# W staged in a room of its own, x loaded in halves, adapter units moved in the order

## The reference

```
x, coeff[8], ids[8], mask[8,1024,1024] (0 or 1), W[1024,1024], bias[1024], weight[8,1024,1024]
output = einsum('bsi,oi->bso', x, W) + bias
sign   = 2*mask - 1
diff   = einsum('bsi,bio->bso', x, sign)
x      = x + output + diff*coeff[b]
x      = x + einsum('bsi,boi->bso', x, weight[ids[b]])
```

## Time and profile before

| | us |
|---|---|
| median of three runs | 422.8 |
| the profiled execution's own time | 423.07 |
| its span, first to last instruction | 421.3 |
| TensorE matmuls busy | 390.4 |
| VectorE busy | 366.6 |
| ScalarE busy | 258.0 |
| TensorE busy from 385.3 to 407.0 | 16.66 of 21.70 |

### The profile page before, as it was taken

How to read it: one execution, slowest core, us unless ns; L and a number is a source line. 1 busy time by engine, 2 the same in 40 slices (tenths; PEclk the granted TensorE clock), 3 DMA queues, 4 the chain that set the end, 5 groups by cost and what they waited for, 6 DMA issues and landing times.

```text
span 421.3 us, 6999 instructions
## 1 busy us (share of the span) xinstructions
PE 390.4 (93%) x2496; PEld 354.8 (84%) x2496; DVE 366.6 (87%) x400; ACT 258.0 (61%) x313; POOL 6.0 (1%) x14
## 2 busy tenths in 40 slices
PE   1979749999999999999999999999999999999777
PEld 1878748999899998999999998999999998999655
DVE  0455899999999999999999999999999999998740
ACT  3476765666676766667566766667566676665321
POOL 1111000000000000000000000000000000000000
PEclk9999979999999999999999999999999999999999
DMA  7998996988579874999779995999479975545211
GB/s 225 273 323 285 226 222 167 276 230 222 167 206 286 252 215 126 269 233 237 188 213 244 231 245 167 281 244 239 148 234 271 248 186 172 155 142 174 83 50 50
DMA packets 62451, 88.54 MB, mean 210 GB/s; under 512 B 7122, under 2 KB 48082, under 8 KB 62418
## 3 DMA queue, kind: packets, MB, share of 16 engines
q1 hardware_dynamic: 62418, 88.11, 78.9%
HBM read 79.70 MB, written 8.39 MB: 209 GB/s over the span
## 4 chain that ended last, share of the span: by engine, by line
PE 66%; DVE 18%; ACT 8%; DMA 3%; issue 2%; SPq 1%; ACTq 0%; DVEq 0%
PE first_ps L243 34%; PE second_ps L260 30%; DVE h_lo L396 6%; DVE natural L380 4%; DVE masks L360 4%; ACT masks L290 3%; DVE M_lo L365 2%; PE turn_ps L227 2%; DMA x_nat<-in_x_dram 2%; DVE w_lo L384 2%; ACT h_hi L316 1%; ACT w_hi L305 1%; DMA natural<-in_L_cond_weight_dram 1%; ACT M_hi L297 1%; ACT out_sb L323 1%
## 5 line engine op out<-in xcount | busy, mean ns | idle before, releaser
L243 PE MATMUL first_ps<-x_lo,M_hi 128*128 128x256 f32 x512 | 147.6, 288 | 10.0 <-DVE h_lo L396 6.0
L243 PE MATMUL first_ps<-x_hi,M_hi 128*128 128x256 f32 x512 | 145.6, 284 | 0.0
L243 PE MATMUL first_ps<-x_hi,M_lo 128*128 128x256 f32 x512 | 145.5, 284 | 0.0
L297 ACT CAST M_hi<-masks 128x1024 fp32r<-128x1024 f32 x64 | 67.2, 1050 | 117.6 <-DVE masks L360 117.6
L243 PEld LDWEIGHTS first_ps<-x_lo,M_hi 128*128 128x128 f32 x512 | 98.9, 193 | 13.2 <-issue 6.2
L260 PE MATMUL second_ps<-w_hi,h_lo 128*128 128x512 f32 x256 | 100.2, 391 | 5.0 <-DVE w_lo L384 2.8
L260 PE MATMUL second_ps<-w_hi,h_hi 128*128 128x512 f32 x256 | 99.9, 390 | 0.0
L243 PEld LDWEIGHTS first_ps<-x_hi,M_hi 128*128 128x128 f32 x512 | 98.9, 193 | 1.1
L260 PE MATMUL second_ps<-w_lo,h_hi 128*128 128x512 f32 x256 | 99.6, 389 | 0.0
L243 PEld LDWEIGHTS first_ps<-x_hi,M_lo 128*128 128x128 f32 x512 | 98.8, 193 | 0.0
L360 DVE SCALAR_TENSOR_TENSOR masks<-masks,coeffs,WT 128x1024 f32<-128x1024 f32 x64 | 81.8, 1278 | 13.0 <-ACT masks L290 9.5
(11 more groups left out here) (16 smaller groups left out, 128.1 us busy)
## 6 DMA issues: line engine op xcount, KB each, us to landing
masks<-in_mask_Bx4096x_ik_dram SPq DMA_DIRECT2D x64, 512.0 KB, 6.6
natural<-in_L_cond_weight_dram SPq DMA_DIRECT2D x256, 128.0 KB, 3.8
x_nat<-in_x_dram SPq DMA_DIRECT2D x8, 1024.0 KB, 7.8
out_dram<-out_sb SPq DMA_DIRECT2D x32, 256.0 KB, 3.3
natural<-in_L_cond_W_dram SPq DMA_DIRECT2D x8, 512.0 KB, 7.8
bias_col<-in_L_cond_b_dram SPq DMA_DIRECT2D x4, 1.0 KB, 5.3
coeffs<-in_condB_coeff_dram SPq DMA_DIRECT2D x1, 4.0 KB, 4.7
ids_row<-in_itok_B_dram SPq DMA_DIRECT2D x1, 0.0 KB
```

Source lines behind the costliest of these rows:

```text
L243: done = nc.tensor.matmul(acc(u), left, right, start=(k == 0 and u % 2 == 0 and j == 0), stop=(k == K - 1 and u % 2 == 1 and j == 2))
L297: nc.scalar.copy(by_chunk(M_hi, n), by_quadrant(masks[:, n % RING, :].bitcast(F32))).then_inc(M_hi_done, 1)
```

## The change

W gets room of its own, `W_nat`, 8 slots that lie where the second halves of `w_hi` and `w_lo` will be (`w_hi` and `w_lo` are each split into a tensor for the even and one for the odd half; the first unit of the odd half, g = 4, waits for all eight turns of W). Loads of W and of the first four units wait for no slot of `natural`. x is loaded, and waited for, in two halves of its columns. On TensorE `first(n)` now stands ahead of `turn_W(n+2)`, and turn_x(b+1, 1) stands at the end of slot 7, ahead of second(b-1, 3); its round and rest stand behind `round_h` and `rest_h`. At the start the second half of the first x is turned after first(0). Units 0 to 3 are formed in slots 4 to 7 (before 5 to 8), slot 8 forms none, and from slot 9 the lag is 5 as before. In slot 63 two units are formed, 58 and 59, and the last four are formed after `rest_h(7)` with the turn of a unit ahead of the rest of the one before. ScalarE copies the last tiles out after the last rounding.

```diff
-        w_hi = sb("w_hi", [P, 2, K, HALF], F32R)
-        w_lo = sb("w_lo", [P, 2, K, HALF], F32R)
+        w_hi_even = sb("w_hi_even", [P, K, HALF], F32R)
+        w_lo_even = sb("w_lo_even", [P, K, HALF], F32R)
+        with nc.sbuf_tensor("W_nat", [P, K, D], F32) as W_nat:
+            pass
+        w_hi_odd = sb("w_hi_odd", [P, K, HALF], F32R)
+        w_lo_odd = sb("w_lo_odd", [P, K, HALF], F32R)
...
+        def unit_of(n):
+            return n - 4 if 4 <= n < 8 else n - 5 if n > 8 else None
... SyncE
             load_mask(0)
-            load_x(0)
-            for n in range(1, RING):
-                load_W(n)
-                load_mask(n)
+            load_x(0, 0)
+            load_W(1)
+            load_mask(1)
+            load_W(2)
+            load_mask(2)
+            load_x(0, 1)
+            load_W(3)
+            load_mask(3)
+            load_W(4)
...
-                if n < RING:
-                    sp.wait_ge(W_turned, n + 1)
-                    load_W(n + RING)
                 if n + RING < CHUNKS:
                     sp.wait_ge(M_done, n + 1)
                     load_mask(n + RING)
-                if n in (4, 5):
-                    for g in (2 * n - 8, 2 * n - 7):
-                        sp.wait_ge(W_turned, RING + g + 1)
-                        load_unit(g)
+                if n < 3:
+                    load_W(n + 5)
+                if n in (2, 3, 4, 5):
+                    load_unit(n - 2)
... TensorE
             turn_W(0)
             turn_x(0, 0)
             turn_W(1)
-            turn_x(0, 1)
-            for n in range(CHUNKS + K):
+            for n in range(CHUNKS):
                 b, i = n // K, n % K
+                first(n)
                 if n + 2 < K:
                     turn_W(n + 2)
-                if n < CHUNKS:
-                    first(n)
-                if i == 0 and 1 <= b < B:
-                    turn_x(b, 1)
+                if n == 0:
+                    turn_x(0, 1)
                 if i == 4 and b + 1 < B:
                     turn_x(b + 1, 0)
+                if i == 7 and b + 1 < B:
+                    turn_x(b + 1, 1)
                 if i % 2 and b:
                     second(b - 1, i // 2)
+            for t in range(4):
+                second(B - 1, t)
... ScalarE
             copy_WT(0)
             sign(0)
+            round_M(0)
             round_x(0, 0)
-            round_M(0)
             copy_WT(1)
             sign(1)
-            round_x(0, 1)
...
                 if n + 1 < CHUNKS:
                     round_M(n + 1)
-                if 0 <= n - W_LAG < CHUNKS:
-                    round_w(n - W_LAG)
+                if n == 0:
+                    round_x(0, 1)
+                if n + 2 < K:
+                    copy_WT(n + 2)
+                if g is not None:
+                    round_w(g)
                 if n + 2 < CHUNKS:
                     sign(n + 2)
-                if n + 2 < K:
-                    copy_WT(n + 2)
-                if i == 2 and 1 <= b < B:
-                    round_x(b, 1)
...
-                if i == 7 and b < B:
+                if n == CHUNKS - 1:
+                    round_w(n - 4)
+                if i == 7:
                     round_h(b)
+                    if b + 1 < B:
+                        round_x(b + 1, 1)
+            take_out(B - 2, 3)
+            for g in range(CHUNKS - 4, CHUNKS):
+                round_w(g)
+            for t in range(4):
+                take_out(B - 1, t)
... VectorE
-                if 0 <= g < CHUNKS - 1:
+                if g is not None:
                     add_diagonal(g + 1)
-                if 0 <= g:
+                    if n == CHUNKS - 1:
+                        turn_w(g + 1)
                     rest_w(g)
-                if i == 2 and 1 <= b < B:
-                    rest_x(b, 1)
+                if n == 0:
+                    rest_x(0, 1)
                 if i == 6 and b + 1 < B:
                     rest_x(b + 1, 0)
-                if i == 7 and b < B:
+                if n == CHUNKS - 1:
+                    rest_w(g + 1)
+                if i == 7:
                     rest_h(b)
+                    if b + 1 < B:
+                        rest_x(b + 1, 1)
+            for g in range(CHUNKS - 4, CHUNKS):
+                add_diagonal(g)
+                turn_w(g)
+                if g > CHUNKS - 4:
+                    rest_w(g - 1)
+            rest_w(CHUNKS - 1)
```

More of the change, by code:

```diff
@@ L17 @@
 RING = 4
-W_LAG = 5
 T_OUT = {3: 0, 5: 1, 7: 2}
@@ L54, in build @@
         M_lo = sb("M_lo", [P, 2, K, P], F32R)
-        w_hi = sb("w_hi", [P, 2, K, HALF], F32R)
-        w_lo = sb("w_lo", [P, 2, K, HALF], F32R)
+        w_hi_even = sb("w_hi_even", [P, K, HALF], F32R)
[4 more added lines that the diff above has]
+        w_lo_odd = sb("w_lo_odd", [P, K, HALF], F32R)
+        w_hi, w_lo = (w_hi_even, w_hi_odd), (w_lo_even, w_lo_odd)
         x_nat = sb("x_nat", [P, ST, D], F32)
@@ L73, in build @@
         mask_loaded = [sem(f"mask_loaded{i}") for i in range(RING)]
-        x_loaded = sem("x_loaded")
+        W_loaded = [sem(f"W_loaded{k}") for k in range(K)]
+        x_loaded = [sem(f"x_loaded{half}") for half in range(2)]
         W_diag_added = sem("W_diag_added")
@@ L168, in _ @@
             sp.wait_ge(ids_loaded, DMA)
-            for n in range(CHUNKS + K + 2):
+            for n in range(CHUNKS + 2):
                 b, i = n // K, n % K
-                if n < RING:
-                    sp.wait_ge(W_turned, n + 1)
-                    load_W(n + RING)
                 if n + RING < CHUNKS:
@@ L185, in _ @@
                 if i == 2 and b + 1 < B:
-                    sp.wait_ge(x_turned, 2 * b + 2)
-                    load_x(b + 1)
+                    for half in range(2):
+                        sp.wait_ge(x_turned, 2 * b + half + 1)
+                        load_x(b + 1, half)
                 if i - 1 in T_OUT and 1 <= b <= B:
@@ L193, in _ @@
                     store(b - 2, 3)
+            for t in range(4):
+                store(B - 1, t)
             for t in range(2):
@@ L256, in second @@
                     for j, (left, right) in enumerate((
-                            (h_lo[:, b % 2, u, rows], w_hi[:, q, u, :]),
-                            (h_hi[:, b % 2, u, rows], w_hi[:, q, u, :]),
-                            (h_hi[:, b % 2, u, rows], w_lo[:, q, u, :]))):
+                            (h_lo[:, b % 2, u, rows], w_hi[q][:, u, :]),
+                            (h_hi[:, b % 2, u, rows], w_hi[q][:, u, :]),
+                            (h_hi[:, b % 2, u, rows], w_lo[q][:, u, :]))):
                         done = nc.tensor.matmul(second_ps[:, t % 2, :], left, right, start=(u == 0 and j == 0),
@@ L401, in _ @@
             add_sum(0)
+            rest_M(0)
             rest_x(0, 0)
[L403 to L407, removed]
+            for n in range(CHUNKS):
+                b, i, g = n // K, n % K, unit_of(n)
                 if n + 1 < CHUNKS:
                     add_sum(n + 1)
-                if 0 <= g:
+                if g is not None:
                     if g == 0:
+                        dve.wait_ge(ident_steps, 2)
                         add_diagonal(0)
```

38 lines of the change are left out of this document (21 added, 17 removed).

## The result

The changed kernel took 425.95 us (median of 20 runs, 423.34 to 430.22) against 423.19 for the kernel before (20 runs on the same chips, 421.49 to 426.23): a ratio of 1.0066, 95% interval 1.0042 to 1.0089. The forecast was 419.5 in a range of 416.3 to 423.2, so the sign was wrong and the time lies outside the range. One of the 20 runs of the changed kernel (430.22), and the profiled execution of the run with unit 1 ahead of x(1) (429.90), belong to a slower state that some executions show, and neither counts in a ratio. The profiled execution of the changed kernel took 428.33, 2.4 us above its median; it shows the pattern, and its sizes are at the long side.

What follows compares the result with a forecast made beforehand. VectorE's own loop of 47.02 us a batch was taken as the bound, TensorE just under it. End -5.5, batches -1.5 and start +3.7 summed to -3.3 us: 419.5 us, range 416.3 to 423.2.

Steps and rivals of the forecast that it cites:

- The end: After the last chunk's first product: TensorE runs through its five last tiles without waiting, -5.5 us.
- F(0): Start of the first product of chunk 0, forecast at 14.35 us.
- S(n): Start of chunk n's sum on VectorE; sums two chunks apart forecast at least 9.6 us apart in the start.
- S(5): Start of the sum of chunk 5 on VectorE, forecast at 38.5 us.
- The step that failed first: In the start: unit 1's load lands close to its use, with about 1 us of cover; otherwise up to 1 us more.
- The batches: Chunk 9 to chunk 57: moving turn_x(b+1, 1) ahead of tile (b-1, 3) shortens VectorE's loop to 46.8 us; -1.5 us.
- rival 1: Clock stays low past the pause before chunk 9's first product: +2.5 us, time 422.0; chance 0.2.
- through both engines: Batch ring through TensorE and VectorE: 46.6 us, under VectorE's loop of 46.8, so x_lo's delay is paid only once.
- the 0.2 us saved on x_hi: In each batch: the x_hi copy runs under rest_h, removing one of VectorE's two 0.2 us waits; loop becomes 46.8.
- Rival 2: The start is quick, at full pace in chunk 0's first product or with the ring at 4.33: -2.1 us, 417.4; chance 0.2.
- Rival 3: x_lo, 1.24 us between rest_h and M_lo(8b+9), is paid in every batch: +8.5 us, time 428; chance 0.1.
- Rival 4: The last tiles are not overlapped, tile (7,2) waiting for unit 63's load or w_lo: 2.8 us, 422.3; chance 0.05.

Runs made afterwards that it cites:

- the two runs on it named under "The start": Changed kernel with turn_W(n+2) ahead of first(n) again, 425.06 us; changed kernel with second half x of batches 1 to 7 back in slot 2, 423.45 us.

## Why the prediction was wrong

**What held.** The end: -5.5 us, with TensorE through from F(63) to the last tile, and with the parts separated it is the same on its own. F(0) came 0.01 us from the forecast, and at 13.98 to 14.08 in three other executions with the same order, so the path to it was right and the last digits luck. Two rounds of S(n) apart: 33.46 - 22.20 = 11.3 where at least 9.6 was said; the excess is F(2) at the low clock, 4.1 us instead of 2.9, and the turn behind it, 1.43 us instead of 1.06, at a granted clock of 0.74. S(5) came out 0.8 us early all the same, because the start up to S(2) was 2.3 us quicker than forecast: two errors that offset each other.

```profile
29.99 1.43 PE L232 MATMUL second_ps<-ident,W_nat 128*128 128x128 f32 x8
```

**The step that failed first** is this one: "Unit 1 lands close to its use (it is asked for behind x(1) and two masks) and has about 1 us of cover under w_hi(0); without it, up to 1 us more." It was wanted at 42.5 and came at 48.7: VectorE waited 6.3 us, 3.5 to 5.0 in three other executions with unit 0 in slot 4 and x(1) ahead of unit 1. The prediction works out no landing time for unit 1; the one pace in its working is 1.6 us for a transfer of 512 KB (328 GB/s), read between 11.0 and 15.9 us, where only masks, x and W were moving. Where units move the engines deliver 205 to 218 GB/s, two thirds of it, and the kernel before shows that too (218 from 45 to 50 us). Moving unit 0 to slot 4 put the diagonal of unit 1, and with it the whole of VectorE's order, in front of a load that was not there. Undoing that alone gave back 4.0 us of the median. Without the wait S(6) would have stood at 43.8, 1.1 us ahead of the forecast; with it, it stood 5.2 behind.

**The second** is "The batches", -1.5 us; measured +1.8. Two parts. F(9) ran at the low clock, 4.61 us instead of 3.13: rival 1, to which 0.2 was given. The window from 75.2 to 79.9 has a clock of 0.64 [above]. The hole before it, 2.3 us of waiting for M_lo(9), is there because turn_x(1,1) no longer fills it and x_lo makes M_lo(9) 1.1 us later. It does not always end so: of the six profiled executions with the turn moved, F(9) took 4.6 us in three and 3.14 in three (x whole, turn_W ahead, the move on top of the end); in none of the seven without the move was it over 3.14, though F(8) ran mostly at the low clock in them. So a chance nearer one half fits what was seen, and the price was 1.5 us, not 2.5. The Trainium skill, "TensorE: Matmul & The Clock Gate", section "Part 1: The HAM clock gate (the 'warmup' mystery)", says that the low clock is the default and that sustained activity releases it; the 4.61 us of F(9) behind two holes agree with that, and the three executions with 3.14 us show that it does not settle this case. From rest_h(0) to F(57) the executions without the move took 288.9 to 289.0 us (six; the seventh, the run with x in slot 2, had a late unit), the moved ones with F(9) at the full clock 290.1 to 291.0, at the low clock 291.8 to 291.9. So the move costs 1.1 us by x_lo and 1.5 by the clock when it is low; the rest, up to 0.9, lies in longer batches further on.

The other part of the 3.3 us is a saving that did not come. The prediction set VectorE's loop at 46.8, and there is a ring that it did not have. It closed "through both engines" over F(8b+15), 46.6 us. But `round_M(n)` waits for first(n-2), since M_hi has two buffers, and ScalarE does round_M(8b+8), round_w, sign and take_out ahead of round_h. In the chain: 265.06 to the end of F(38) at 299.9 (34.8), to rest_h(4) at 304.14 (4.3), to F(41) at 312.09 (7.95) is 47.03. The x_lo that was moved behind rest_h made TensorE late enough for that wait to bind, so the 0.2 us saved on x_hi came back. That the ring, and not VectorE's loop, sets the 47.03 is read from the chain and not shown by a run with a third M_hi buffer, which was not tried. It matters little: with the turn put back, and the ring's wait gone, the batch was 47.02, VectorE's loop as before.

**Rival 2** (a quick start) came true in part and bought nothing: F(0) took 3.13 us, the full pace (4.0 and 4.7 in two other executions with the same order), and S(2) was at 22.20 instead of 24.5; the time went into F(2) at the low clock and into the wait for unit 1. **Rival 3** did not: x_lo was paid once, and the batches behind the first were 47.0 to 47.3. That the first was over the 47.3 which was to be its sign comes from F(9)'s clock. **Rival 4** did not.

**Summed by parts** in medians: the end -5.5; against it the early units +4.0 and the moved half x +2.5, each from its own run on the changed kernel and each with an interval clear of the changed kernel's. The turn behind the first product adds 0.9, which is inside the interval and so not shown. The three together gave 8.8, more than their sum of 7.4; the difference is within what the intervals allow. 8.8 - 5.5 is 3.3; the changed kernel is 2.8 above the kernel before.

**The version to keep** is the kernel before with the end alone, 417.88 us, 1.5% under it, with the fewest edits; no other run was shown to beat it.

## What to carry to other kernels

When work is moved ahead in an engine's order, the load under it must be priced at the rate of the stretch in which it will move, with all that is then in flight, not at the rate of a quieter one; a transfer that is late there stops everything behind it. List every semaphore wait of every engine that the shift touches, those that have never cost anything too: a buffer with two places is a ring, and a 1.2 us shift was enough to close it, here at no cost in time. A small job that stands between two dependent ones can be what keeps TensorE's clock up: moving the 0.9 us turn left the next product at the low clock in three of six executions, and in none of seven where it stayed. Look where the hole goes before moving it. And measure the parts apart: a change that lost 0.7% held one that wins 1.5%.

## What the runs showed of the hardware that was not expected

The low clock returned behind holes much shorter than the one of 6 us in the kernel before. F(2) began after a wait of 2.2 us, did its first matmuls 0.12 us apart and fell to 0.21 apart from 27.4 us on; F(4), behind a wait of 2.1 us, ran slowly too. With turns and products spaced by such waits the clock was 0.74 from 25 to 30 and 0.76 from 35 to 40, with TensorE busy 82% and 59% of these stretches; in the kernel before, from 5 to 54 us, it read 1.00, though it has a hole of 2.8 us before 51.5. Without their longest, the runs of the changed kernel spread over 5.8 us, the 20 of the kernel before over 4.7. The mean granted clock does not tell them apart: 0.972 to 0.988 in the changed kernel's runs, 0.975 to 0.992 in all but one (0.946) of the kernel before's in the series of the experiments. Which hole falls to the low clock in which run is not told by the times. The slow pace of the first turns in the kernel before (1.97 us for eight at 11.0) stood beside a granted clock of 1.00 in the records, so in the first microseconds the pace of the matmuls says more than the clock column.

Asking for a load earlier hardly made it land earlier. Unit 1's last quarter went out at 41.9 and landed at 46.5 in the kernel before; it went out 6 to 7 us earlier and landed between 45.7 and 48.7 in the changed kernel and the two runs on it named under "The start". The rate was about the same meanwhile: from 40 to 45 us 225 GB/s in the kernel before, 205 in the changed one, 231 in the run with turn_W ahead.
